# The first stage of a fused adaLN block in halves of the batch element: loads in order of use, statistics beside the modulation products, shift and scale rows spread by a matmul of ones

## What is computed

```python
mod = (silu(c) @ wmod).reshape(4, 6, 1, 256)      # c: 4x256, wmod: 256x1536
sa, ca, ga, sb, cb, gb = (mod[:, k] for k in range(6))
ga = sign(ga) * max(|ga|, 0.25)                   # the same for gb
h = layernorm(x) * (1 + ca) + sa
n = h * rsqrt(mean(h * h) + eps)                  # then q, k, v of 16 heads of 64
x = x + ga * (causal attention, softmax over the query axis, and W_o)
h = layernorm(x) * (1 + cb) + sb
x = x + gb * (one of 16 experts by argmax, capacity 256, 256 -> 1024 -> 256)
```

## Time and profile before

| what | value |
|---|---|
| median of 3 runs | 1390.43 us (1387.12 to 1391.08) |
| the profiled execution's own time | 1391.48 us |
| span of its profile | 1389.7 us, 24022 instructions |
| PE busy | 1230.4 us (89%) |
| DVE busy | 824.3 us (59%) |
| ACT busy | 573.8 us (41%) |
| POOL busy | 326.1 us (23%) |
| granted TensorE clock, mean | 0.945 of full |
| HBM read, written | 94.76 MB, 48.00 MB |

### The profile page before, as it was taken

How to read it: one execution, slowest core, us unless ns; L and a number is a source line. 1 busy time by engine, 2 the same in 40 slices (tenths; PEclk the granted TensorE clock), 3 DMA queues, 4 the chain that set the end, 5 groups by cost and what they waited for, 6 DMA issues and landing times.

```text
span 1389.7 us, 24022 instructions
## 1 busy us (share of the span) xinstructions
PE 1230.4 (89%) x7256; PEld 863.6 (62%) x7256; DVE 824.3 (59%) x2166; ACT 573.8 (41%) x1387; POOL 326.1 (23%) x487
## 2 busy tenths in 40 slices
PE   2588888888999999999999999999988529999995
PEld 0455555555666666666666666666656528888884
DVE  4465665666666676676767666666655623444443
ACT  0354554554555555555555554555541001111110
POOL 2221112111223333222232212212212520111111
PEclk8788999999999999999999999999998759999998
DMA  5311111111221222121222211112257852565630
GB/s 195 129 66 58 66 57 65 65 38 42 69 80 57 72 75 81 55 68 64 72 67 65 87 54 60 60 68 68 69 189 246 272 194 87 194 234 173 234 103 18
DMA packets 99118, 139.55 MB, mean 100 GB/s; under 512 B 9848, under 2 KB 71162, under 8 KB 98808
## 3 DMA queue, kind: packets, MB, share of 16 engines
q1 hardware_dynamic: 90504, 113.81, 25.1%
q10 hardware_dynamic: 4464, 16.25, 2.9%
q0 software_dynamic: 4096, 8.82, 1.6%
HBM read 94.76 MB, written 48.00 MB: 103 GB/s over the span
## 4 chain that ended last, share of the span: by engine, by line
PE 68%; issue 11%; ACT 6%; DVE 5%; DMA 4%; POOL 3%; SPq 2%; DVEq 0%; ACTq 0%; POOLq 0%
PE SC L653 16%; PE Z L671 14%; PE Z L818 8%; PE SC L792 8%; ACT E L853 5%; PE XA L625 5%; PE XA L703 4%; PE XA L635 3%; PE XB L635 3%; PE XB L625 3%; DMA xln<-in_x 2%; POOL Wvl L1347 1%; PE XB L690 1%; DMA out<-th 1%; DVE nm L1065 1%
## 5 line engine op out<-in xcount | busy, mean ns | idle before, releaser
L853 ACT ACTIVATE E<-SC,nm 128x512 f32<-128x512 f32 (+7 forms) x512 | 375.5, 740 | 425.5 <-DVE nm L1065 425.5
L1065 DVE CUSTOM_DVE_ANT_0 SC<-SC,mask 128x512 f32<-128x512 f32 (+7 forms) x512 | 376.0, 787 | 203.5 <-PE SC L653 202.4
L653 PE MATMUL SC<-XQ,XK 64*128 64x512 f32 (+3 forms) x2304 | 270.3, 367 | 56.1 <-ACT E L853 54.7
L653 PEld LDWEIGHTS SC<-XQ,XK 64*128 64x128 f32 x2304 | 187.8, 191 | 156.0 <-issue 138.9
L671 PE MATMUL Z<-E,vs 128*64 128x512 f32 (+3 forms) x1536 | 271.6, 496 | 3.0 <-DVE vs L1043 3.0
L671 PEld LDWEIGHTS Z<-E,vs 128*64 128x64 f32 x1536 | 100.4, 138 | 140.5 <-issue 127.9
L818 PE MATMUL Z<-W,hh 128*128 128x256 f32 x512 | 114.9, 383 | 2.2 <-DVE yb L1311 2.2
L792 PE MATMUL SC<-bT,W 128*128 128x256 f32 x512 | 114.5, 383 | 0.0
L818 PEld LDWEIGHTS Z<-W,hh 128*128 128x128 f32 x512 | 97.3, 192 | 15.6 <-DVE yb L1311 2.6
L792 PEld LDWEIGHTS SC<-bT,W 128*128 128x128 f32 x512 | 98.4, 192 | 13.6
L853 ACT ACTIVATION_READ_ACCUMULATOR E<-SC,nm 128x1 f32 x512 | 101.2, 198 | 0.0
(11 more groups left out here) (193 smaller groups left out, 1719.8 us busy)
## 6 DMA issues: line engine op xcount, KB each, us to landing
W<-in_w SPq DMA_DIRECT2D x32, 1024.0 KB, 8.4
z_s<-zs ACTq DMA_DIRECT2D x31, 512.0 KB, 2.6
zt<-z_s SPq DMA_DIRECT2D x24, 512.0 KB, 3.8
W<-in_wqk SPq DMA_DIRECT2D x33, 257.0 KB, 2.7
slots_s<-zt SPq DMA_DIRECT2D x16, 520.0 KB, 4.0
xb<-slots_s SPq DMA_DIRECT2D x16, 520.0 KB, 3.7
xb<-xh_s SPq DMA_DIRECT2D x24, 256.0 KB, 4.4
Wv<-in_wv SPq DMA_DIRECT2D x17, 256.0 KB, 2.7
```

What stands on the lines that cost most here:

```text
L653: last = pe.matmul(SC[h][:, at:at + z - a], XK[rows, ap, kp, lo:lo + P], XQ[rows, ap, qp, a:z], start=(t == 0), stop=(t == 2))
L853: act.activation(E[:, h, EOFF[kb]:EOFF[kb + 1]], SC[h][:, at:at + S - lo], ACT.Exp, bias=nm[:, h, kb:kb + 1], scale=-1.0, accum_out=rs[:, ...
L1065: dve.tensor_tensor_reduce(SC[h][:, at:at + S - lo], SC[h][:, at:at + S - lo], mask[:, 0:S - lo], 1.0, BIG, ALU.add, ALU.min, nm[:, h, kb: ...
```

## The change

The computation is the same. What moves:

- **Loads.** wmod is loaded in two column pieces, first the 512 columns of the first shift and scale (`mod_lead`), the other 1024 later. x comes in two halves of 4 tiles, ahead of `W`. `cT` has a semaphore of its own (`c_in`), for which alone ACT waits.
- **Products.** PE makes the first 512 columns into XA. DVE takes both rows for all 4 batch elements. PE spreads batch element 0's two rows over 128 partitions by a product of a row of ones (`one`) with them, into XB. The other 1024 columns go into Z.
- **Statistics** stand on DVE behind the first two rows, by halves, and POOL's power too. The scale and shift of batch element 0 are read from XB instead of `modB`.
- **The other four rows** (second shift and scale, both gates) are taken behind that, the two gates in one instruction each time; the rows lie in `E` and no longer in `V`.
- **The way over DRAM** is made twice: first 2 rows (loads for batch elements 1 to 3), then the other 4 rows, with one load for each batch element.
- POOL splits `W` behind the two powers, and `Wv` behind the RMS factors. PE waits for the second low part only before the second half of q.

```diff
             start_counters(sp, [*post_out])
-            sp.dma_start(cT[:, :], c_d).then_inc(mod_in, 16)
-            sp.dma_start(wmod[:, 0:6 * D], wmod_d[0]).then_inc(mod_in, 16)
-            sp.dma_start(wmod2[:, 0:6 * D], wmod_d[1]).then_inc(mod_in, 16)
+            sp.dma_start(cT[:, :], c_d).then_inc(c_in, 16)
+            sp.dma_start(wmod[:, 0:2 * D], wmod_d[0][:, 0:2 * D]).then_inc(mod_lead, 16)
+            sp.dma_start(wmod2[:, 0:2 * D], wmod_d[1][:, 0:2 * D]).then_inc(mod_lead, 16)
+            sp.dma_start(xw[:, 0:TPB // 2, :], x_d[0:TPB // 2].rearrange("t p d -> p t d")).then_inc(xw_lead, 16)
+            sp.dma_start(xw[:, TPB // 2:TPB, :], x_d[TPB // 2:TPB].rearrange("t p d -> p t d")).then_inc(xw_in, 16)
             sp.dma_start(W[:, :], wqk_d[0]).then_inc(w_in, 16)
+            sp.dma_start(wmod[:, 2 * D:6 * D], wmod_d[0][:, 2 * D:6 * D]).then_inc(mod_in, 16)
+            sp.dma_start(wmod2[:, 2 * D:6 * D], wmod_d[1][:, 2 * D:6 * D]).then_inc(mod_in, 16)
             sp.dma_start(Wv[:, :], wv_d[0]).then_inc(wv_in, 16)
-            sp.dma_start(xw, x_d[0:TPB].rearrange("t p d -> p t d")).then_inc(xw_in, 16)
-            sp.wait_ge(mod_rows, 6)
-            sp.dma_start(mod_s, modr).then_inc(mod_out, 16)
+            sp.wait_ge(mod_rows, 2)
+            sp.dma_start(mod_s[:, 0:2 * D], modr[:, 0:2 * D]).then_inc(mod_out, 16)
             sp.wait_ge(mod_out, 16)
...
+            for b in range(1, B):
+                sp.dma_start(modB[:, b, 0:2, :].rearrange("p k d -> p (k d)"),
+                             mod_s[b:b + 1, 0:2 * D].broadcast_to([P, 2 * D])).then_inc(modb0_in, 16)
+            sp.wait_ge(mod_rows, 5)
+            sp.dma_start(mod_s[:, 2 * D:6 * D], modr[:, 2 * D:6 * D]).then_inc(mod_out, 16)
+            sp.wait_ge(mod_out, 32)
+            for b in range(B):
+                sp.dma_start(modB[:, b, 2:6, :].rearrange("p k d -> p (k d)"),
+                             mod_s[b:b + 1, 2 * D:6 * D].broadcast_to([P, 4 * D])).then_inc(modb_in, 16)
             sp.dma_start(bvB[:, :], bv_d.broadcast_to([P, PAIRS * P])).then_inc(const_in, 16)
...
+            modulate(XA[:, :], 0)
+            pe.wait_ge(mod_rows, 2)
             pe.wait_ge(consts, 5)
+            pe.wait_ge(one_set, 1)
+            pe.matmul(XB[:, :], one[:, :], modr[0:1, 0:2 * D], start=True, stop=True).then_inc(mod_spread, 1)
+            pe.wait_ge(mod_in, 32)
+            for k in (1, 2):
+                modulate(Z[:, (k - 1) * HALF:k * HALF], k)
...
-            pe.wait_ge(wide_lo, 2)
+            pe.wait_ge(wide_lo, 1)
             pe.wait_ge(const_in, 64)
...
-            act.wait_ge(mod_in, 48)
+            act.wait_ge(c_in, 16)
...
+            dve.tensor_copy(modr[:, 0:D], XA[0:B, 0:D]).then_inc(mod_rows, 1)
+            dve.tensor_scalar(modr[:, D:2 * D], XA[0:B, D:2 * D], 1.0, None, ALU.add).then_inc(mod_rows, 1)
...
+                dve.tensor_scalar(wve[:, tiles], wmv[:, tiles, 1], LN_EPS, None, ALU.add).then_inc(wide_ve, 1)
+            spread = XB[:, :].rearrange("p (k d) -> p k d", k=2)
+            dve.wait_ge(mod_spread, 1)
...
+            dve.wait_ge(mod_mm, 3)
+            dve.tensor_copy(taken[:, SB - 2, :], raw[:, SB - 2, :]).then_inc(mod_rows, 1)
+            dve.tensor_scalar(taken[:, CB - 2, :], raw[:, CB - 2, :], 1.0, None, ALU.add).then_inc(mod_rows, 1)
+            dve.tensor_scalar(sgn[:, 0, :, :], gate_in, 0.0, 2.0, ALU.is_ge, ALU.mult).then_inc(setup, 1)
...
+            dve.tensor_tensor(gate_out, sgn[:, 0, :, :], sgn[:, 1, :, :], ALU.mult).then_inc(mod_rows, 1)
```

More of the change, by code:

```diff
@@ L289, in adaln_block @@
         sc = sb("sc", [P, NC * B], stack=att)
-        modr = V[0:B, :, :, :].rearrange("p a b c -> p (a b c)")[:, 0:6 * D]
-        sgn = zs[0:B, 0:2 * D].rearrange("p (a d) -> p a d", a=2)
+        one = hn[0:1, 0:P]
+        modr = E[0:B, 1, 2 * S:2 * S + 6 * D]
+        sgn = zs[0:B, 0:4 * D].rearrange("p (a g d) -> p a g d", a=2, g=2)
         blank = zt[:, :, :, :].rearrange("p a c t -> p (a c t)")[:, 0:FILL * ROW]
@@ L619, in project @@
                         pe.wait_ge(auxa_free, st.n("auxa"))
+                    if isinstance(st.j, int) and st.g < 0 and (kind, half) == ("q", 1):
+                        pe.wait_ge(wide_lo, 2)
                     if kind in "qk":
@@ L951, in _ @@
             dve.memset(mhalf[:, :], -0.5).then_inc(consts, 1)
+            dve.memset(one[:, :], 1.0).then_inc(one_set, 1)
             dve.wait_ge(mod_mm, 1)
[L954 to L972, removed]
@@ L975, in _ @@
[L975 to L984, removed]
@@ L990, in _ @@
+            spread = XB[:, :].rearrange("p (k d) -> p k d", k=2)
+            dve.wait_ge(mod_spread, 1)
+            for half, tiles in enumerate(halves):
+                dve.wait_ge(wide_rs, half + 1)
+                for t in range(half * TPB // 2, (half + 1) * TPB // 2):
+                    dve.tensor_scalar(hw[:, t, :], xw[:, t, :], wmv[:, t, 0:1], wrs[:, t:t + 1], ALU.subtract, ALU.mult).then_inc(wide, 1)
                 dve.wait_ge(wide, 2 * TPB + (half + 1) * TPB // 2 + half)
-                dve.tensor_tensor(hw[:, tiles, :], hw[:, tiles, :], modB[:, 0, CA, :].unsqueeze(1).broadcast_to([P, TPB // 2, D]),
+                dve.tensor_tensor(hw[:, tiles, :], hw[:, tiles, :], spread[:, CA:CA + 1, :].broadcast_to([P, TPB // 2, D]),
@@ L992, in _ @@
                                   ALU.mult).then_inc(wide, 1)
-                dve.wait_ge(wide, 3 * TPB + half + 1)
-                dve.tensor_tensor(hw[:, tiles, :], hw[:, tiles, :], modB[:, 0, SA, :].unsqueeze(1).broadcast_to([P, TPB // 2, D]),
+                dve.wait_ge(wide, 2 * TPB + (half + 1) * (TPB // 2 + 1))
+                dve.tensor_tensor(hw[:, tiles, :], hw[:, tiles, :], spread[:, SA:SA + 1, :].broadcast_to([P, TPB // 2, D]),
                                   ALU.add).then_inc(wide_h, 1)
+            raw = Z[0:B, :].rearrange("p (k d) -> p k d", k=4)
@@ new lines, in _ @@
+            dve.tensor_scalar(sgn[:, 0, :, :], sgn[:, 0, :, :], -1.0, None, ALU.add).then_inc(setup, 1)
+            dve.tensor_scalar(sgn[:, 1, :, :], gate_in, -1.0, 0.25, ALU.mult, ALU.max).then_inc(setup, 1)
+            dve.wait_ge(setup, 5)
+            dve.scalar_tensor_tensor(sgn[:, 1, :, :], gate_in, 0.25, sgn[:, 1, :, :], ALU.max, ALU.max).then_inc(setup, 1)
+            dve.wait_ge(setup, 6)
+            dve.tensor_tensor(gate_out, sgn[:, 0, :, :], sgn[:, 1, :, :], ALU.mult).then_inc(mod_rows, 1)
@@ L1366, in step @@
                 if st.has("post"):
+                    if st.b == 1:
+                        pool.wait_ge(modb_in, 64)
                     bt = st.tile // TPB
@@ L1396, in step @@
                         split_values_weights(st.b * COUPLES + st.j + 2)
+            minus_halves = mhalf[:, :].broadcast_to([P, TPB])
+            pool.wait_ge(consts, 5)
+            for half in range(2):
+                tiles = slice(half * TPB // 2, (half + 1) * TPB // 2)
+                pool.wait_ge(wide_ve, half + 1)
+                pool.tensor_tensor(wrs[:, tiles], wve[:, tiles], minus_halves[:, tiles], ALU.pow).then_inc(wide_rs, 1)
             pool.wait_ge(w_in, 16)
```

40 lines of the change are left out of this document (21 added, 19 removed).

## The result

The changed kernel took 1384.12 us (median of 14 runs, 1380.05 to 1389.05); the kernel before, with the runs that were added beside it, 1387.22 us (median of 14, 1384.6 to 1391.19). The two medians alone are 3.1 us apart; the ratio is not simply that of the medians, and the text says which of the two it uses. The forecast was 1385.9 us, a gain of 4.5.

What follows compares the result with a forecast made beforehand. It took the first step's start as the bound, set by queued loads of constants, then xln: low part of q at 42.6 for 47.13 us. That 4.5 us off the 1390.43 median gave 1385.9, range 1382.5 to 1390.0.

Steps and rivals of the forecast that it cites:

- What sets the moment: Start of the first step: VectorE's low part of q waits on SyncE's queue for constants, then xln; 42.6 for 47.13 us.
- The early chain: First stage on TensorE and VectorE: first product at 5.8 us for 9.22, 128x1024 operations done at 21.3, late rows at 25.1.
- The DMA chain: SyncE's queue behind the second store at 25.1 us: last constant landed at 36.4, xln at 41.6.
- short broadcasts are slow: Rival: broadcast loads with 4 KB rows run at 300 GB/s; gain only 2.4 us, 1388.0 us; chance 0.14.
- The estimate by the Trainium skill, DMA: Bandwidth & Descriptors, section Anatomy of one DMA: 2.0 us plus bytes over 436 GB/s for the 4.48 MB: xln landed at 39.5, gain 6.6 us, 1383.8 us.
- What the steps give through: Steps and experts behind the first stage: its gain comes out at the end as it is, 4.5 us.
- the rival on the clock: TensorE idles, and half clock lasts three more product groups at 1.25 us each; gain 0.8 us, 1389.7 us; chance 0.12.
- Faster by over 0.3%: Outcome for the whole kernel: gain above the bound of 4.2 us; chance 0.48.
- within 0.3%: Outcome for the whole kernel: change inside the bound of 4.2 us; chance 0.45.

Runs made afterwards that it cites:

- e4: The changed kernel with four more 512 KB broadcast loads into unused buffers ahead of the constants; ratio 1.0018 to the kernel before.
- e3: The changed kernel with the four constant loads and the first xln load both issued right behind Wv at the start; ratio 0.9915 to the kernel before.
- e1: The changed kernel with only the four constant loads issued right behind Wv at the start; ratio 0.9947 to the kernel before.
- e2: The changed kernel with only the first xln load issued right behind Wv at the start; ratio 0.9954 to the kernel before.
- e5: The kernel before, not the changed one, with the four constant loads and the first xln load issued early; ratio 1.0007 to the kernel before.
- e10: The changed kernel run and profiled once more, with no edit; ratio 0.9973 to the kernel before.
- e7: The changed kernel with unread products, 13 ahead of TensorE's wait for the constants and 6 behind q's first half; ratio 0.9972 to the kernel before.
- e6: e3 with the four late rows and their way over DRAM moved into the first step; ratio 0.9899 to the kernel before.
- e9: e6 with the late rows split in two parts and five unread products behind the second part of the modulation products; ratio 0.9892 to the kernel before.

## Why the prediction was right

**What sets the moment.** Right, and shown from four sides: more bytes ahead of the constants push everything back (e4), both loads early pull it forward (e3), each alone does a small part (e1, e2), and in the kernel before the same two edits do nothing (e5).

**The early chain.** Nearly right. The first product started at 5.02, not 5.8: the first piece landed at 4.89 (1.86 + 3.03), for 5.5 by the count and 5.8 as I took it. From there VectorE's chain held to within 0.1: the last shift ended at 20.5, 15.5 us behind the first product as in the sum, and the store was issued 19.24 us behind it (24.26), for 19.3. Scale and shift from PSUM cost the same 1.22, as the PSUM operand in the earlier trace rows had it. Two errors didn't show: the second part of wmod was there at 13.2 and not at 12, hidden behind VectorE, and from the first RMS scaling to both low parts it took 8.0 us (25.46 to 33.43) for 7.0, which the constants hid.

**The DMA chain** came out at the right place through errors that cancel. The late rows were ready 0.8 us before the 25.1 of the sum (24.26), and the way over DRAM took 1.7 us for 2.06: together 1.2 us early. The 2.78 MB up to the last constant took 11.4 us from the first load's issue at 25.99, where the sum had 9.2: 2.2 us more. `woT`, `W`, `Wv` and `xln` (1.7 MB) then went faster than the sum had them: `xln` landed 4.0 us behind the constants, for 5.2, and the window from 36.5 to 41.5 shows 402 GB/s where the sum took 396 for `woT` and the middle of 205 and 396 for the rest. So -1.2, +2.2 and -1.2: `xln` at 41.33 for 41.6, low part at 42.31 for 42.6. The sum was inside its bounds, the 2.2 us by themselves were not; that the three cancel to 0.3 us is luck.

The 2.2 us are the price of the rival "short broadcasts are slow" (2.1), but not by its mechanism. The window from 27 to 31 shows 253 GB/s and the next one 388, and in e4 loads with the same rows of 4 KB went at 417 right behind an equally slow start. So the length of the row isn't what made it slow; the delay lies in the first 4 us behind the pause of the queue. What causes it no run shows.

The estimate by the Trainium skill, DMA: Bandwidth & Descriptors, section Anatomy of one DMA, would have had `xln` land 12.3 us behind the first load. It took 15.3 (25.99 to 41.33). The fit in that section of the Trainium skill is for a single DMA of the kind that GpSimd issues, and here 12 DMAs stand on SyncE's queue, so the difference doesn't contradict it.

**What the steps give through.** The prediction said that what the first stage gives comes out at the end as it is. That holds only roughly. The 4.8 us at the low part were 4.1 at the first score, 3.2 near 350 us and 2.5 in the span, against 3.9 by the ratio. In e10, the same kernel, 4.6 at the low part were 4.8 at the first score and 1.1 near 350 us, against 3.8 by the ratio. Counted against before's one profile, the others win up to 0.6 us (e7) or lose up to 3.5 (e10) between the low part and 350 us. From there to the last of these statistics, near 748 us, before, changed and e10 take 396.9, 396.9 and 397.2 us: nothing is gained or lost. TensorE's mean granted clock is 0.92, 0.92 and 0.90 from 60 to 350 us, and 1.00 in all three from 350 to 745. That the clock makes the difference fits this but is not shown.

Over all kernels gain and position go together: 12.2 us at the low part gave 11.8 by the ratio (e3), 15.4 gave 14.0 (e6), -0.7 gave -2.5 (e4). They don't in e5, where faster products of the first groups made the lead: its 2.4 us at the first score gave nothing.

The 0.7 us between low part and first score went where the rival on the clock had it: k's and q's second group took 5.5 us at half clock (0.50 from 43 to 48) for 4.8. That rival was bigger (a gain of only 0.8 us left) and its size a guess; the runs bear it out only in part, since the same kernel did the two groups in 4.6 in e10. What decides whether the clock comes back during k's group, the two profiles leave open.

**The absolute time.** The forecast of 1385.9 us was counted from 1390.43, the median of three runs of before. The median of 14 is 1387.22. Had the sum started there, it would have given 1382.7, and the measured 1384.12 would have lain 1.4 above it instead of 1.8 below. The forecast is to be judged by its gain, 4.5 for 3.9 (3.1 between medians).

**The chance.** The gain forecast lay 0.3 us above the line of 0.3% and the measured one 0.3 us below. "Faster by over 0.3%" had 0.48 and did not come; "within 0.3%" had 0.45 and did. Between two cases so near each other the chances said little.

## What to carry to other kernels

When a stage is shortened, put the two chains side by side, engines and queue, and name what the first consumer behind it will wait for next; here 12 us could be won at the first step's low part (e3), and 7 of them were left in a wait for four constants and one tile that depended on nothing. A load without dependencies belongs ahead of the first wait of its queue, and two such loads have to be moved together, since each hides the other. The version to build on is e6, 14 us faster than before by the ratio and 12.6 between medians; e9 is no slower, but the times don't tell the two apart. Filling TensorE's idle stretches moved single groups by 1 to 2 us and nothing that the time could show.

## What the runs showed of the hardware

The spread of a kernel's own runs (9.0 us over the 14 of the changed kernel, 6.6 over the 14 of before) goes with TensorE's mean granted clock: over the changed kernel's 14 runs the correlation is -0.72, with 1380.05 and 1380.49 us at 0.948 and 0.950, and 1386.53 and 1389.05 at 0.942. That is a correlation and no cause. But a change of a few us in the first stage is measured against a larger spread from run to run.

Broadcast loads of 512 KB that follow a pause of the queue started slowly: 253 GB/s from 27 to 31 us and then 388 in the changed kernel, 251 and then 417 with four more such loads (e4). At the very start of the kernel two loads of 256 KB landed 2.9 us behind their issue in the median, while the load of 512 KB issued right behind them, x's first half, took 6.2.
